# First attention: probabilities scaled on ScalarE, the score factor moved into the queries' evictions

## The chip, the cores and the metric

The kernel runs on one core of a Trainium2 chip. The metric is the device time of one execution in microseconds. A run of one execution more was taken with the hardware profiler; all rows below are from it.

## The reference, cut to what matters

Four decoder layers run one after the other on x (4 sequences of 256 tokens, width 512) with a context of 64 tokens for each sequence. The change touches the first attention only:

```python
hidden = jnp.concatenate([context, latents], axis=1)
q = (latents @ Wq.T).reshape(b, q_len, H, HD)          # 16 heads of 96
k = (hidden @ Wk.T).reshape(b, s_len, KV, HD)          # 4 key heads, 320 keys
v = (hidden @ Wv.T).reshape(b, s_len, KV, HD)
scale = 1.0 / jnp.sqrt(jnp.asarray(HD, q.dtype))
scores = jnp.einsum('bkgqd,bksd->bkgqs', q, k) * scale
attn = jax.nn.softmax(scores.astype(jnp.float32), axis=-1).astype(q.dtype)
out = jnp.einsum('bkgqs,bksd->bkgqd', attn, v)
```

Later layers (feed-forwards, two more kinds of attention, two mixtures of experts, and a last feed-forward whose weights are first quantised to a table of 16 values) are computed by code that stays as it is.

## The kernel before

All work is written as one list of steps (`schedule`), and every engine walks this list in its order, doing its own part of each step and waiting on semaphores for the others. No engine overtakes: what stands behind a waiting instruction waits too.

The first attention is cut into 64 units of one head and one sequence (256 queries, two tiles of 128, by 320 keys). Eight stages hold 8 units each: four groups of heads for the first two sequences, then for the other two. Unit n goes through a pipeline over four steps of the list:

- `scores0` n: TensorE multiplies queries by keys into two PSUM banks. VectorE takes the negated maximum of each row of both (L1192), multiplies the two maxima by the factor HD0 ** -0.5 (L1195, a 128x2 operation) and marks `max0`. ScalarE waits for that mark, then takes the exponential of both banks with the same factor as its scale (L936), writes `e0`, and accumulates the row sums in `sm`.
- `scale0` n stands one unit later, behind `scores0` n + 1. VectorE takes the reciprocal of the two sums (L1200) and multiplies the two tiles of `e0` in place by it (L1202, 128x320 each), marking `probs0`.
- `turn0` n stands behind `scores0` n + 2: TensorE transposes the probabilities (L1718, L1719), and ScalarE copies them out of PSUM to `eT0` (L944, L946).
- `pv0` n stands behind `scores0` n + 3: TensorE multiplies by the values (L1728). ScalarE writes the rounded high part of the result over the queries in `q0` (L888, 96x256), and VectorE the low part, which is the rest (L1118, 96x256). The low part waits for the high part.

Between the units stand the projections of the next stage: the queries (`q0`, four products of 12 matrix multiplications with 512 columns, evicted as a high part by ScalarE, L888 96x512, and a low part by VectorE, L1118 96x512), the keys, and the output projection of the stage before (`o0`, added to x on L1214). A stage's first two or three units have no projection of queries beside them, so TensorE has least to do there.

Two kinds of other work are woven in. The first is the splitting of weights into a high part (ScalarE, L903) and a low part (POOL, L813, 2 to 2.6 us each). The second is the quantisation of the last layer's weights, named `nf`: VectorE makes steps of a staircase (L1581 `nf_y`, L1575, L1591), which TensorE sums (L1977). Their places in the list are fixed by counting costs that the change leaves alone.

TensorE's banks go round a ring of 7, and a bank is claimed again only after its last reader. In the light units the transpose of unit n claims the banks of the scores of unit n + 1, whose last readers are the exponentials of that unit.

Of the kernel before, what the change touches and what calls it, by code (L numbers as in the profile page):

```python
# [5 lines left out]
FP32 = mybir.dt.float32  # L6
F32R = mybir.dt.float32r
INT32 = mybir.dt.int32
ALU = mybir.AluOpType
ACT = mybir.ActivationFunctionType  # L10
# [11 lines left out]
TPB = S // P  # L22
H0, G0, HD0 = 16, 4, 96
HPG = H0 // G0
KEYS0 = S + CTX
# [14 lines left out]
E0_RING = 5  # L40
# [308 lines left out]
def build(nc, a, out, known, only=None):  # L349
    ctx = ExitStack()  # L350
    with ctx:
        sig = Signals(nc, ctx, known)

        def sb(name, shape, dt, scope=ctx):
            return scope.enter_context(nc.sbuf_tensor(name, shape, dt))
# [13 lines left out]
        mx = sb("mx", [P, 4, 2 * HPC], FP32)  # L369
        sm = sb("sm", [P, 4, 2 * HPC], FP32)  # L370
# [13 lines left out]
        q0 = sb("q0", [HD0, 2, 2, HPG, HALF], F32R, s0)  # L384
        k0 = sb("k0", [HD0, 2, 2, BPH, KEYS0], F32R, s0)
        v0 = sb("v0", [P, TPH + BPH, G0 * HD0], FP32, s0)
        eT0 = sb("eT0", [P, 2, 3, S], FP32, s0)
        e0 = sb("e0", [P, E0_RING, KEYS0], FP32, s0)
# [78 lines left out]
        def psum(key):  # L467
            return banks[sig.bank_for(key)]
# [133 lines left out]
        if known:  # L602
            last = known.last_step
            free_after = {}
            slot_of, n = {}, 0
# [45 lines left out]
        slot_no, n = {}, 0  # L651
# [13 lines left out]
        def weight(name, part):  # L665

            _, p, dims, _, dest, _ = chunks[chunk_no[name]]
            if dest is not None:
                return dest[part]
            size = int(np.prod(dims))  # L670
            return flat(slots[0:p, slot_no[name] % NSLOT, part, 0:size], dims)
# [118 lines left out]
        def split_source(i):  # L790
            _, p, dims, *_ = chunks[i]
            return flat(staging[0:p, i % 2, 0:int(np.prod(dims))], dims)
# [3 lines left out]
        def _(pool):  # L796
# [12 lines left out]
            def split(i):  # L809
                pool.wait_ge(*sig.when("weight_high", i))  # L810
                _, p, dims, *_ = chunks[i]
                hi, lo = weight(chunks[i][0], 0), weight(chunks[i][0], 1)
                g.tensor_tensor(lo, split_source(i), hi.bitcast(FP32), ALU.subtract).then_inc(*sig.mark("weight_low", i))  # L813
# [68 lines left out]
        def _(act):  # L882
            sc = nc.scalar

            def high(stage, key, dst, src, product=None, func=ACT.Copy, **kw):

                act.wait_ge(*sig.when(*(product or (f"{stage}_product", key))))
                sc.activation(dst, src, func, **kw).then_inc(*sig.mark(f"{stage}_high", key))  # L888
# [37 lines left out]
                high("kc0", s, k0[:, s % 2, 0, :, S:], psum(("kc0", s))[0:HD0, 0:BPH * CTX].rearrange("p (b n) -> p b n", b=BPH))  # L926

            def q0_(s, h):
                high("q0", (s, h), q0[:, s % 2, 0, h], psum(("q0", s, h))[0:HD0])

            def scores0(n, s, bl, h):
                act.wait_ge(*sig.when("max0", n))
                for i in range(TPB):
                    if 2 * n + i >= E0_RING:
                        act.wait_ge(*sig.when("turn0_product", (2 * n + i - E0_RING) // 2))
                    sc.activation(e0[:, (2 * n + i) % E0_RING], psum(("scores0", n, i))[:, 0:KEYS0], ACT.Exp, scale=HD0 ** -0.5,  # L936
                                  bias=mx[:, n % 4, 2 + i:3 + i], accum_out=sm[:, n % 4, i:i + 1])\
                        .then_inc(*sig.mark("exp0", (n, i)))

            def turn0(n, s, bl, h):  # L940
                act.wait_ge(*sig.when("turn0_product", n))
                if n >= 2:
                    act.wait_ge(*sig.when("pv0_product", n - 2))
                sc.activation(eT0[:, n % 2, 0:2], psum(("turn0", n, 0))[:].rearrange("p (k n) -> p k n", k=2),  # L944
                              ACT.Copy).then_inc(*sig.mark("turn0_kept", (n, 0)))
                sc.activation(eT0[0:CTX, n % 2, 2], psum(("turn0", n, 1))[0:CTX, 0:S],  # L946
                              ACT.Copy).then_inc(*sig.mark("turn0_kept", (n, 1)))
# [136 lines left out]
            def nf_turn(m):  # L1084
                for i in range(2):
# [3 lines left out]
                    elif i == 0:  # L1089
                        act.wait_ge(*sig.when("nf4_max", (0, 0)))  # L1090
                    sc.activation(nf_t[0:88, i], psum(("nf_turn", m))[0:88, i * P:(i + 1) * P], ACT.Copy)\
                        .then_inc(*sig.mark("nf4_turned", (m, i)))

            handlers = {"split": split, "turn": turn, "v0": v0_, "k0": k0_, "kc0": kc0_, "q0": q0_, "scores0": scores0,
                        "turn0": turn0, "pv0": pv0, "up0": up0, "down0": down0, "scores1": scores1, "pv1": pv1, "bias2": bias2,
                        "route1": route1, "router1": router1, "zt1": zt1, "k2": k2_, "m2": m2_, "c2": c2_,
                        "gate2": gate2, "moe": moe, "hid2": hid2, "k3": k3_, "v3": v3_, "q3": q3_,
# [7 lines left out]
        def _(dve):  # L1105
            v = nc.vector
            links = [0]

            def link(ins):

                links[0] += 1
                ins.then_inc(sig.sem("vector_chain"), 1)
                dve.wait_ge(sig.sem("vector_chain"), links[0])

            def low(stage, key, dst, src, hi):

                dve.wait_ge(*sig.when(f"{stage}_high", key))
                v.tensor_tensor(dst, src, hi.bitcast(FP32), ALU.subtract).then_inc(*sig.mark(f"{stage}_low", key))  # L1118
# [65 lines left out]
                    psum(("kc0", s))[0:HD0, 0:BPH * CTX].rearrange("p (b n) -> p b n", b=BPH), k0[:, s % 2, 0, :, S:])  # L1184

            def q0_(s, h):
                low("q0", (s, h), q0[:, s % 2, 1, h], psum(("q0", s, h))[0:HD0], q0[:, s % 2, 0, h])

            def scores0(n, s, bl, h):
                for i in range(TPB):  # L1190
                    dve.wait_ge(*sig.when("scores0_product", (n, i)))
                    ins = v.tensor_reduce(mx[:, n % 4, i:i + 1], psum(("scores0", n, i))[:, 0:KEYS0], AX.X, ALU.max,  # L1192
                                          negate=True)
                link(ins)
                v.tensor_scalar(mx[:, n % 4, 2:4], mx[:, n % 4, 0:2], HD0 ** -0.5, None, ALU.mult)\  # L1195
                    .then_inc(*sig.mark("max0", n))

            def scale0(n):
                dve.wait_ge(*sig.when("exp0", (n, TPB - 1)))
                link(v.reciprocal(sm[:, n % 4, 2:4], sm[:, n % 4, 0:2]))  # L1200
                for i in range(TPB):
                    v.tensor_scalar(e0[:, (2 * n + i) % E0_RING], e0[:, (2 * n + i) % E0_RING], sm[:, n % 4, 2 + i:3 + i], None, ALU.mult)\  # L1202
                        .then_inc(*sig.mark("probs0", (n, i)))

            def pv0(n, s, bl, h):
                cs = slice(bl * S, (bl + 1) * S)
# [377 lines left out]
            def nf_end(n, m, f):  # L1584
# [3 lines left out]
                if m == 2:  # L1588
                    o, code, i1 = o.rearrange("p (q r) -> p r q", r=4), code.rearrange("p (r q) -> p r q", r=4), \
                        i1.rearrange("p (r q) -> p r q", r=4)  # L1590
                v.scalar_tensor_tensor(o, code, float(STAIR_SCALE), i1, ALU.mult, ALU.mult).then_inc(*sig.mark("nf4_dequantised", n))  # L1591

            handlers = {"stats": stats, "turn": turn, "k0": k0_, "kc0": kc0_, "q0": q0_, "scores0": scores0,
                        "scale0": scale0, "scale3": scale3, "pv0": pv0, "o0": o0, "up0": up0, "down0": down0, "scores1": scores1,
                        "pv1": pv1, "router1": router1, "route1": route1, "z1": z1, "zt1": zt1, "b1": b1, "k2": k2_,
                        "m2": m2_, "bias2": bias2, "gate2": gate2, "moe": moe, "hid2": hid2, "out2": out2,
                        "values3": values3, "scores3": scores3, "pv3": pv3, "o3": o3, "up3": up3,
                        "down3": down3, "nf_max": nf_max_, "nf": nf, "nf_end": nf_end}
# [463 lines left out]
```

## Time and profile before

| what | value |
|---|---|
| median of 3 runs | 1707.35 us (1707.07 to 1708.24) |
| the profiled execution | 1711.2 us, its span 1709.4 us |
| TensorE busy | 1443.9 us, 84% of the span |
| VectorE busy | 1083.9 us, 63% |
| ScalarE busy | 458.6 us, 27% |
| POOL busy | 296.5 us, 17% |
| mean granted TensorE clock | 0.893 |
| the units of the first attention | 65.8 us to 622 us of the span |

The span is the time from the first to the last instruction. TensorE is busy for most of it. The first attention takes a third of the span, and all that the change touches lies there. In the rows DVE is VectorE, ACT is ScalarE, PE is TensorE, and PEld its weight loads.

### The profile page before, as it was taken

To read this page: it belongs to the slowest core of one execution; us is meant where nothing else is said; L and a number is where in the kernel's file an instruction comes from. 1 tells how busy PE (TensorE), PEld (TensorE's weight loads), DVE (VectorE), ACT (ScalarE), POOL (GpSimd) and SP (SyncE) were. 2 spreads that over 40 slices of the span, in tenths; PEclk is the share of its full clock that TensorE was granted. 3 is DMA by queue.
4 is the path that set the end of the run, shared out by engine and by line. 5 is a ranking of instruction groups with operands and counts; after the bars stand their busy time and mean duration, and the time that the engine had idled before them with its cause. 6 is when DMAs were issued, how large, how long until landed. Compare 5 with 4: busy or idle time off the path is not lost.

```text
span 1709.4 us, 18898 instructions
## 1 busy us (share of the span) xinstructions
PE 1443.9 (84%) x6489; PEld 1131.2 (66%) x6489; DVE 1083.9 (63%) x2489; ACT 458.6 (27%) x994; POOL 296.5 (17%) x170
## 2 busy tenths in 40 slices
PE   6569999998999898899646878858999778789998
PEld 5347776776677667688545767747887546567786
DVE  4556876767777666948886756554446399944142
ACT  3223423332343333313131202101221333322010
POOL 4101111111111111202021002111543121012120
PEclk9779999999999999999855699557999889899999
DMA  5521232322232212222001112200112000001011
GB/s 184 159 77 46 80 82 68 82 74 58 64 89 71 75 50 69 72 66 67 25 26 46 42 40 60 63 18 1 50 49 62 26 25 1 1 27 60 16 36 49
DMA packets 99407, 96.40 MB, mean 56 GB/s; under 512 B 13138, under 2 KB 72418, under 8 KB 99314
## 3 DMA queue, kind: packets, MB, share of 16 engines
q1 hardware_dynamic: 98802, 94.35, 19.0%
q8 instruction: 54, 0.88, 0.2%
q0 software_dynamic: 512, 0.85, 0.2%
q14 instruction: 39, 0.32, 0.1%
HBM read 84.34 MB, written 10.82 MB: 56 GB/s over the span
## 4 chain that ended last, share of the span: by engine, by line
PE 62%; DVE 25%; issue 4%; ACT 4%; DMA 2%; SPq 1%; POOL 1%; DVEq 0%; ACTq 0%; POOLq 0%
PE bank L1636 48%; PE bank L1977 5%; PE bank L1728 4%; DVE nf_y L1581 3%; DVE st L1141 2%; DVE xn L1159 1%; PE bank L1661 1%; DVE xT L1118 1%; PE bank L1718 1%; DVE mx L1192 1%; DVE mx L1498 1%; ACT e L936 1%; DMA nf_w<-in_L_w 1%; DVE sm L1510 1%; SPq L767 1%
## 5 line engine op out<-in xcount | busy, mean ns | idle before, releaser
L1636 PE MATMUL bank<-xT,slots 128*128 128x512 f32 (+1 forms) x1920 | 467.6, 402 | 9.6 <-DVE xT L1118 7.8
L1636 PEld LDWEIGHTS bank<-xT,slots 128*128 128x128 f32 (+1 forms) x1920 | 354.8, 186 | 109.0 <-issue 8.9
L813 POOL TENSOR_TENSOR slots<-staging,slots 128x1024 fp32r<-128x1024 f32 (+4 forms) x97 | 230.5, 2379 | 1103.0 <-ACT slots L903 1103.0
L1581 DVE TENSOR_SCALAR nf_y<-nf_w 128x512 fp32r<-128x512 f32 (+2 forms) x495 | 232.2, 496 | 29.0 <-PE bank L1977 28.0
L1636 PE MATMUL bank<-slots,h 128*128 128x512 f32 (+1 forms) x728 | 178.8, 405 | 20.1 <-DVE h L1248 13.9
L1977 PE MATMUL bank<-nf_y,nf_d 128*128 128x512 f32 (+2 forms) x495 | 170.6, 429 | 10.3 <-DVE nf_y L1581 8.0
L1636 PEld LDWEIGHTS bank<-slots,h 128*128 128x128 f32 (+1 forms) x728 | 140.8, 194 | 56.1 <-DVE h L1248 14.8
L903 ACT ACTIVATE slots<-staging 128x1024 fp32r<-128x1024 f32 (+4 forms) x97 | 98.1, 1018 | 189.9 <-PE bank L1636 174.2
L936 ACT ACTIVATE e<-bank,mx 128x320 f32<-128x320 f32 x128 | 66.4, 523 | 271.1 <-DVE mx L1195 254.0
L1977 PEld LDWEIGHTS bank<-nf_y,nf_d 128*128 128x128 f32 (+1 forms) x495 | 95.3, 197 | 47.0 <-issue 15.5
L1214 DVE TENSOR_TENSOR x<-bank,x 128x512 f32<-128x512 f32 x72 | 49.7, 690 | 110.9 <-PE bank L1636 110.6
L1728 PE MATMUL bank<-eT,v 128*96 128x256 f32 (+1 forms) x384 | 112.0, 414 | 1.5 <-ACT eT L946 1.5
L1118 DVE TENSOR_TENSOR q<-bank,q 96x256 fp32r<-96x256 f32 (+1 forms) x96 | 48.8, 508 | 77.3 <-ACT q L888 76.8
L1636 PE MATMUL bank<-slots,q 96*128 96x512 f32 x384 | 95.3, 397 | 0.7 <-DVE q L1118 0.7
L1718 PE MATMUL bank<-ident,e 128*128 128x128 f32 x256 | 50.6, 294 | 44.5 <-ACT e L936 22.4
L1636 PEld LDWEIGHTS bank<-slots,q 96*128 96x128 f32 x384 | 71.6, 188 | 18.6 <-issue 2.1
L1728 PEld LDWEIGHTS bank<-eT,v 128*96 128x96 f32 (+1 forms) x384 | 58.2, 172 | 37.6 <-issue 25.3
L1661 PE MATMUL bank<-ident,xn 128*128 128x128 f32 x256 | 49.6, 360 | 31.9 <-DVE xn L1159 31.6
L1636 PE MATMUL bank<-k,q 96*128 96x320 f32 x384 | 69.6, 317 | 5.7 <-ACT e L936 4.4
L1718 PEld LDWEIGHTS bank<-ident,e 128*128 128x128 f32 x256 | 35.0, 151 | 53.7 <-ACT e L936 30.6
L1636 PEld LDWEIGHTS bank<-k,q 96*128 96x128 f32 x384 | 61.9, 192 | 13.0 <-ACT e L936 4.7
L1661 PEld LDWEIGHTS bank<-ident,xn 128*128 128x128 f32 x256 | 42.8, 189 | 39.2 <-issue 34.7
(246 smaller groups left out, 1897.8 us busy)
## 6 DMA issues: line engine op xcount, KB each, us to landing
staging<-in_L_wqkT SPq DMA_DIRECT2D x16, 480.0 KB, 3.8
nf_out<-nf_w SPq DMA_DIRECT2D x30, 256.0 KB, 2.1
staging<-nf_out SPq DMA_DIRECT2D x30, 256.0 KB, 2.8
staging<-in_L_woT SPq DMA_DIRECT2D x16, 384.0 KB, 3.5
staging<-in_L_w SPq DMA_DIRECT2D x12, 512.0 KB, 4.0
nf_a<-nf_max SPq DMA_DIRECT2D x40, 128.0 KB, 3.6
nf_r<-nf_rcp SPq DMA_DIRECT2D x40, 128.0 KB, 3.4
nf_w<-in_L_w SPq DMA_DIRECT2D x15, 256.0 KB, 4.4
```

The lines of the kernel that those rows point to most:

```text
L813: g.tensor_tensor(lo, split_source(i), hi.bitcast(FP32), ALU.subtract).then_inc(*sig.mark("weight_low", i))
L903: sc.activation(weight(name, 0), split_source(i), ACT.Copy).then_inc(*sig.mark("weight_high", i))
L936: sc.activation(e0[:, (2 * n + i) % E0_RING], psum(("scores0", n, i))[:, 0:KEYS0], ACT.Exp, scale=HD0 ** -0.5, bias=mx[:, n % 4, 2 + i:3 + ...
L1118: v.tensor_tensor(dst, src, hi.bitcast(FP32), ALU.subtract).then_inc(*sig.mark(f"{stage}_low", key))
L1141: ins = v.bn_stats(st[:, t], x[:, t])
L1214: v.tensor_tensor(x[:, t], src, x[:, t], ALU.add).then_inc(*sig.mark(*mark))
L1581: v.tensor_scalar(nf_y[0:rows, i % STAIR_RING, 0:size], w_, bound, first, compare, ALU.mult)\
L1636: ins = mm(dst, l_, r_, start=i == 0, stop=i == len(passes) - 1)
L1661: ins = nc.tensor.transpose(bank[:, i * P:(i + 1) * P], xn[:, i, c * P:(c + 1) * P], ident[:])
L1718: nc.tensor.transpose(b0[:, (2 * k + i) * P:(2 * k + i + 1) * P], e0[:, (2 * n + i) % E0_RING, k * P:(k + 1) * P], ident[:])
L1728: ins = mm(bank[0:HD0, 0:S], v0[0:p, t, g * HD0:(g + 1) * HD0], eT0[0:p, n % 2, k], start=k == 0, stop=k == 2)
L1977: mm(banks[NF_BANK][0:rows, 0:size], nf_d[0:rows, j - 1, 0:rows], nf_y[0:rows, i % STAIR_RING, 0:size], start=j == 1, stop=j == NPART).the ...
```

## The change

Four things differ. ScalarE's eviction of the queries multiplies by HD0 ** -0.5, and VectorE's low part of the queries does the same in one operation with two steps, so that the scores come out of the product already scaled. The 128x2 multiplication of the maxima is gone, and the second maximum itself marks `max0`. The exponential has no scale any more. VectorE keeps only the reciprocal of `scale0` and marks `sums0`, and ScalarE multiplies the two tiles of `e0` in place (new function `scale0`, with a factor per row as the scale of a copy).

```diff
             def q0_(s, h):
-                high("q0", (s, h), q0[:, s % 2, 0, h], psum(("q0", s, h))[0:HD0])
+                high("q0", (s, h), q0[:, s % 2, 0, h], psum(("q0", s, h))[0:HD0], scale=HD0 ** -0.5)
...
-                    sc.activation(e0[:, (2 * n + i) % E0_RING], psum(("scores0", n, i))[:, 0:KEYS0], ACT.Exp, scale=HD0 ** -0.5,
-                                  bias=mx[:, n % 4, 2 + i:3 + i], accum_out=sm[:, n % 4, i:i + 1])\
+                    sc.activation(e0[:, (2 * n + i) % E0_RING], psum(("scores0", n, i))[:, 0:KEYS0], ACT.Exp,
+                                  bias=mx[:, n % 4, i:i + 1], accum_out=sm[:, n % 4, i:i + 1])\
                         .then_inc(*sig.mark("exp0", (n, i)))
+
+            def scale0(n):
+                act.wait_ge(*sig.when("sums0", n))
+                for i in range(TPB):
+                    e = e0[:, (2 * n + i) % E0_RING]
+                    sc.activation(e, e, ACT.Copy, scale=sm[:, n % 4, 2 + i:3 + i]).then_inc(*sig.mark("probs0", (n, i)))
...
             def q0_(s, h):
-                low("q0", (s, h), q0[:, s % 2, 1, h], psum(("q0", s, h))[0:HD0], q0[:, s % 2, 0, h])
+                dve.wait_ge(*sig.when("q0_high", (s, h)))
+                v.scalar_tensor_tensor(q0[:, s % 2, 1, h], psum(("q0", s, h))[0:HD0], HD0 ** -0.5,
+                                       q0[:, s % 2, 0, h].bitcast(FP32), ALU.mult, ALU.subtract).then_inc(*sig.mark("q0_low", (s, h)))
...
-                link(ins)
-                v.tensor_scalar(mx[:, n % 4, 2:4], mx[:, n % 4, 0:2], HD0 ** -0.5, None, ALU.mult)\
-                    .then_inc(*sig.mark("max0", n))
+                ins.then_inc(*sig.mark("max0", n))
 
             def scale0(n):
                 dve.wait_ge(*sig.when("exp0", (n, TPB - 1)))
-                link(v.reciprocal(sm[:, n % 4, 2:4], sm[:, n % 4, 0:2]))
-                for i in range(TPB):
-                    v.tensor_scalar(e0[:, (2 * n + i) % E0_RING], e0[:, (2 * n + i) % E0_RING], sm[:, n % 4, 2 + i:3 + i], None, ALU.mult)\
-                        .then_inc(*sig.mark("probs0", (n, i)))
+                v.reciprocal(sm[:, n % 4, 2:4], sm[:, n % 4, 0:2]).then_inc(*sig.mark("sums0", n))
```

TensorE's and POOL's orders stay the same. On ScalarE, this is the order around unit 32 (the first unit of the fifth stage) before: the two exponentials of unit 32, the two copies of the transposed probabilities of unit 30, and the high part of the product with the values of unit 29.

```order
L936 ACTIVATE e0,sm<-bank2,mx 128x320
L936 ACTIVATE e0,sm<-bank3,mx 128x320
L944 ACTIVATE eT0<-bank4 128x512
L946 ACTIVATE eT0<-bank5 64x256
L888 ACTIVATE q0<-bank6 96x256
L903 ACTIVATE slots<-staging 128x960
```

The same place of the changed kernel:

```order
L936 ACTIVATE e0,sm<-bank2,mx 128x320
L936 ACTIVATE e0,sm<-bank3,mx 128x320
L944 ACTIVATE e0<-e0,sm 128x320 x2
L950 ACTIVATE eT0<-bank4 128x512
L952 ACTIVATE eT0<-bank5 64x256
L888 ACTIVATE q0<-bank6 96x256
L903 ACTIVATE slots<-staging 128x960
```

The two multiplications of unit 31's probabilities have come in between the exponentials and the evictions (L950 and L952 are the old L944 and L946).

On VectorE, this is the same unit before: the maxima of unit 32, a step of the staircase, the reciprocal of unit 31's sums, and the low part of unit 29's product with the values.

```order
L1192 TENSOR_REDUCE mx<-bank2 128x1
L1192 TENSOR_REDUCE mx<-bank3 128x1
L1195 TENSOR_SCALAR mx<-mx 128x2
L1581 TENSOR_SCALAR nf_y<-nf_w 128x512
L1200 RECIPROCAL sm<-sm 128x2
L1202 TENSOR_SCALAR e0<-e0,sm 128x320 x2
L1581 TENSOR_SCALAR nf_y<-nf_w 128x512
L1118 TENSOR_TENSOR q0<-bank6,q0 96x256
```

The same place of the changed kernel:

```order
L1200 TENSOR_REDUCE mx<-bank2 128x1
L1200 TENSOR_REDUCE mx<-bank3 128x1
L1584 TENSOR_SCALAR nf_y<-nf_w 128x512
L1206 RECIPROCAL sm<-sm 128x2
L1584 TENSOR_SCALAR nf_y<-nf_w 128x512
L1124 TENSOR_TENSOR q0<-bank6,q0 96x256
```

The multiplication of the maxima and the two of the probabilities are gone, and the reciprocal still stands behind a step of the staircase.

## Rows read from the trace of the kernel before

**Rows 1.** Busy time by stretch, us; light units 268:284, heavy ones 284:334, sum over 60:620

```profile
268.00:284.00 16.00, 12.75 (x61) 8.84 (x60) 14.13 (x32) 6.99 (x21) 4.39 (x2) 0.89 0.22 67
284.00:334.00 50.00, 50.00 (x246) 37.80 (x245) 34.49 (x85) 15.68 (x45) 4.23 (x2) 1.00 0.29 76
...
sum 560.00, PE 500.89 PEld 371.97 DVE 395.38 ACT 195.13 POOL 73.71; mean PE 26.36 PEld 19.58 DVE 20.81 ACT 10.27 POOL 3.88
```

**Rows 2.** The chain that ended last, units 40 and 41: start, us, what

```profile
429.54 0.18 DVE mx L1195
...
430.17 0.70 ACT e L936 x3
430.87 0.49 ACT eT L944
...
431.61 0.28 ACT q L888
...
431.91 0.42 DVE q L1118
```

**Rows 3.** The same chain: first and last of 16 short L1195, and of 5 long

```profile
84.53 0.18 DVE mx L1195
...
205.63 1.27 DVE mx L1195
...
500.68 1.82 DVE mx L1195
...
613.14 0.18 DVE mx L1195
```

**Rows 4.** The same chain: where it passes VectorE's scaling of e

```profile
69.76 0.68 DVE e L1202 x2
...
80.64 0.68 DVE e L1202 x2
```

**Rows 5.** VectorE's groups, 60:620: count, busy us, mean ns, idle before, releaser

```profile
L1581 DVE TENSOR_SCALAR nf_y<-nf_w 128x512 fp32r<-128x512 f32 x324 | 160.9, 520 | 10.7 <-PE bank L1977 9.9
...
L1202 DVE TENSOR_SCALAR e<-e,sm 128x320 f32<-128x320 f32 x128 | 43.7, 384 | 2.3
L1118 DVE TENSOR_TENSOR q<-bank,q 96x256 fp32r<-96x256 f32 x62 | 26.1, 421 | 54.4 <-ACT q L888 53.9
```

**Rows 6.** ScalarE's groups by shape, whole span, same columns

```profile
L888 ACT ACTIVATE xT<-bank 128x512 fp32r<-128x512 f32 x56 | 30.1, 599 | 26.3 <-PE bank L1661 26.1
L888 ACT ACTIVATE q<-bank 96x256 fp32r<-96x256 f32 x64 | 24.0, 375 | 3.3 <-PE bank L1728 3.1
...
L888 ACT ACTIVATE xT<-bank,lnw 128x512 fp32r<-128x512 f32 x8 | 5.4, 687 | 7.6 <-PE bank L1661 6.5 <-DMA lnw<-in_L_lnw 1.1
...
L920 ACT ACTIVATE v<-bank 128x384 f32<-128x384 f32 x8 | 3.7, 488 | 12.4 <-PE bank L1636 12.4
...
L1024 ACT ACTIVATE bqw<-bqf 128x512 fp32r<-128x512 f32 x1 | 0.6, 629 | 4.0 <-DVE bqf L1373 4.0
```

**Rows 7.** ScalarE in time: two 128x64 with a factor per row, together

```profile
955.16 0.59 ACT L1001 ACTIVATE r<-r,rs 128x64 f32<-128x64 f32 x2 [1.91 <-DVE rs L1330]
```

**Rows 8.** VectorE's groups, whole span: without and with a factor on the PSUM input

```profile
L1214 DVE TENSOR_TENSOR x<-bank,x 128x512 f32<-128x512 f32 x72 | 49.7, 690 | 110.9 <-PE bank L1636 110.6
...
L1216 DVE SCALAR_TENSOR_TENSOR x<-bank,x 128x512 f32<-128x512 f32 x8 | 5.5, 691 | 12.8 <-PE bank L1636 12.8
```

**Rows 9.** All engines in time, unit 32: start, us, what, idle before

```profile
335.80 2.57 POOL L813 TENSOR_TENSOR slots<-staging,slots 96x1024 fp32r<-96x1024 f32 x1 [16.78 <-ACT slots L903]
...
337.00 1.40 DVE L1195 TENSOR_SCALAR mx<-mx 128x2 f32<-128x2 f32 x1
...
338.31 0.41 DVE L1581 TENSOR_SCALAR nf_y<-nf_w 128x512 fp32r<-128x512 f32 x1
...
338.65 0.15 DVE L1200 RECIPROCAL sm<-sm 128x2 f32<-128x2 f32 x1
...
339.45 0.60 ACT L944 ACTIVATE eT<-bank 128x512 f32<-128x512 f32 x1
```

More of the change, by code:

```diff
@@ L1092, in nf_turn @@
                         .then_inc(*sig.mark("nf4_turned", (m, i)))
-            handlers = {"split": split, "turn": turn, "v0": v0_, "k0": k0_, "kc0": kc0_, "q0": q0_, "scores0": scores0,
+            handlers = {"split": split, "turn": turn, "v0": v0_, "k0": k0_, "kc0": kc0_, "q0": q0_, "scores0": scores0, "scale0": scale0,
                         "turn0": turn0, "pv0": pv0, "up0": up0, "down0": down0, "scores1": scores1, "pv1": pv1, "bias2": bias2,
```

## The prediction, made before the changed kernel was run

> **What bounds the kernel now.** I first read the busy time by stretch. TensorE is busy for 500.89 of the 560 us of the first attention, VectorE for 395.38, ScalarE for 195.13 [rows 1]. Taken over everything, ScalarE has plenty of room and VectorE is the busier of the two. But the stretches differ. In 284:334, a stage's heavy units with their projections, TensorE is busy for all 50.00 us, and neither engine is on the path. In 268:284, where a stage begins and TensorE has little to do, it is busy for 12.75 of 16 us, and the granted clock falls to 0.89. What VectorE and ScalarE cost the kernel, they cost there.
>
> So I read the chain of waits in those places next, piece by piece. Rows 2 are one crossing of it. VectorE multiplies the maxima, ScalarE does two exponentials, then the two evictions of the transposed probabilities, then the high part of the product with the values, and only then can VectorE do the low part, the staircase steps and the next maxima. From the end of L1195 at 429.72 to the start of L1118 at 431.91 the chain is on ScalarE for 2.19 us, and none of it on VectorE's scaling of e, which runs meanwhile. I counted how often the chain goes from L1195 to ScalarE in this way: 16 times with the short L1195 of 0.18 us, and 5 times with one of 1.27 to 1.82 us, 7.6 us together [rows 3]. VectorE's scaling of e stands on the chain in full only twice, 0.68 us each [rows 4].
>
> The group rows say the same over all units: VectorE sat idle for 54.4 us before 62 low parts, 53.9 of it for ScalarE's high part [rows 5]. That is 0.88 us in a unit. VectorE comes to this place early and waits for ScalarE.
>
> **The change part by part.**
>
> *Taken off VectorE.* The two scalings cost 2 x 0.34 us of its time in a unit (0.68 us for the pair [rows 4]), the multiplication of the maxima 0.18 us and a 0.02 us hand-over [rows 2]. Over 64 units that is 56 us. Where TensorE is the bound this is worth nothing. In the crossings the scaling is hidden behind ScalarE, and VectorE will only wait longer before L1118: about 0.88 + 0.68 + what is added on ScalarE. What does count there is the multiplication, since ScalarE waits for it: 0.20 us a crossing.
>
> *Put on ScalarE.* No row has this copy, so I build it. From PSUM with a constant scale, 256 columns take 375 ns and 384 take 488, so 320 take 431 [rows 6]. A factor per row adds 687 - 599 = 88 ns, and an input in SBUF in place of PSUM 629 - 599 = 30 ns [rows 6]: 549 ns for one. Back to back they overlap: two 340 ns operations of 128x64 with a pointer end in 0.59 us, so 90 ns are shared [rows 7]. That gives 0.46 us a copy, 0.92 us a pair. The lower bound is the PSUM form with a constant, overlapped: 0.34, a pair 0.68. The upper bound is 0.55 with no overlap: a pair 1.10. I take 0.92, since each addend has a row of its own.
>
> The Trainium skill, page "ScalarE: Activation LUTs", section "Rules for kernel authors", sends multiplications to VectorE, which speaks against the change. The rows agree for this shape: 0.34 us a tile on VectorE against my 0.46 on ScalarE.
>
> *Where the pair stands.* It is behind the exponentials and ahead of the evictions and of the high part that VectorE waits for. All of it lies on the chain in a crossing. Queued behind it are L950, L952, the high part on L888, and sometimes a split of weights, and POOL and the DMA queue wait for that. The new wait for `sums0` costs nothing in most units: the reciprocal stands behind one staircase step of about 0.34 us, and is done before the two exponentials are.
>
> *Short crossings.* 0.92 - 0.20 = +0.72 us. 16 of them: +11.5 us. In three of these, read further, the chain goes on to TensorE's transposes and not to an eviction. Three of the six transposes can run after the first copy, under most of the second's 0.46 us. I take off 3 x 0.33 = 1.0 us.
>
> *Long crossings.* Here L1195 was held. In rows 9 POOL's subtraction runs from 335.80 to 338.37, L1195 is issued at 337.00 and ends at 338.40, where the same instruction takes 0.18 us elsewhere. The rule in the Trainium skill, page "SBUF — State Buffer", section "Who interferes with whom", is that VectorE in a two-port mode and POOL lock each other out for a whole instruction. The trace agrees. By that rule alone one would say that all five holds come back.
>
> They don't, by the order: the next instruction on VectorE is a step of the staircase, and the reciprocal stands behind it. Such steps are held as well: their mean is 520 ns [rows 5], where one alone takes 0.41 us [rows 9]. In unit 32 the exponentials would start at about 337.0 and end at 338.0. The staircase step would still begin to move only when POOL ends, and the reciprocal end at about 338.80, as before. ScalarE then waits for it, copies until 338.82 + 0.92 = 339.74, and starts the eviction that before started at 339.45. That is +0.29 us. 5 of them: +1.5 us.
>
> *Pieces that go.* The 0.68 us at 80.64 goes. At 69.76 the pair goes too, but ScalarE must then do exponentials, copies and the next exponentials in a row, which takes the same time to about 0.1 us. Together -0.8 us.
>
> *The queries.* 32 evictions get a constant factor. On VectorE, 128x512 with a factor takes 691 ns against 690 without [rows 8]. Zero. The exponential loses an immediate: zero.
>
> **Sum:** 11.5 - 1.0 + 1.5 - 0.8 = +11.2 us, against the profiled execution 1711.2 + 11.2. Its own time is 3.9 us over the median of the runs, and I apply the difference to the median: 1707.35 + 11.2 = 1718.5 us. With a pair at 0.68: 16 x 0.48 - 1.0 + 5 x 0.05 - 0.8 = +6.1, 1713.5. With a pair at 1.10: 16 x 0.90 - 1.0 + 5 x 0.47 - 0.8 = +15.0, 1722.4. This case's own range is 1713 to 1723.
>
> **The rivals.**
>
> *The holds come back.* If the staircase step is not held where the multiplication was, for instance because POOL now starts later against it, the five long crossings give 0.92 - 0.20 - 1.34 (7.6 / 5 - 0.18) = -0.62 each instead of +0.29: 11.2 - 4.6 = +6.6, 1714. This is what the rule on the Trainium skill's page "SBUF — State Buffer" gives if it is applied to the multiplication alone. Against it: the same step is next in the order at unit 32, and POOL's start is set by ScalarE's split ahead of the unit. Chance 0.10.
>
> *No change.* ScalarE is busy for 195 of 560 us, and the copies vanish in its idle time. That is true of the heavy units. For the light ones it would need TensorE to be the later one at the crossings, and the chain says otherwise. With a pair near 0.68 and the holds back, 6.1 - 5 x (0.05 + 0.86) = +1.5 us: 1709. Chance 0.13.
>
> *Faster.* VectorE is the bound in the light units by its own work, and each of the 21 crossings gives back what was taken from it, 0.88 us: -18.5 us, 1689. It decides from the point where VectorE has no idle time ahead of L1118. For it: VectorE is busy for 14.13 of the 16 us in 268:284 [rows 1]. Against it: the 54.4 us [rows 5], and that rows 2 have ScalarE between two pieces of VectorE. Chance 0.08.
>
> *Slower still.* TensorE idles longer in each crossing and its clock falls more often. In 268:284 the clock of 0.89, with levels of 2.4 and 1.2 GHz, is 3.5 us of 16 at the lower one, and costs about 1.8 us. Four or five such falls more add 8 us: 1727. Chance 0.09.
>
> **How the numbers follow.** The forecast case has 0.60, all between 1713 and 1723. With the holds back (0.10) or the clock (0.09) it is slower too: slower 0.79, same 0.13, faster 0.08. Within 0.2%, 3.4 us, is about what a measurement of this kernel can't tell from no change. The range takes in the no-change case in part and the clock case: 1708.5 to 1727.
>
> **What would show it.** In the changed profile: new groups of 128 copies of about 550 ns on ScalarE's L944, and in pairs 1.0 us. VectorE's busy time down by about 56 us less holds, and its idle time before the 96x256 low parts up from 54.4 us to some 150 us (62 x 1.6 us more). ScalarE's busy time up by some 60 us. TensorE idle longer where the stages begin, and TensorE's busy time at the full clock unchanged. On the chain L944's copies 20 times or more, between the exponentials and the evictions. At unit 32, an idle time of ScalarE behind the exponentials that ends with the reciprocal. The prediction is wrong if the chain at the crossings shows VectorE's own work on both sides, if the copies come out below 0.3 us, or if the long `nf_y` steps shrink with the holds.

## The result, and the profile after

The changed kernel takes 1729.89 us (median of 4 runs, 1727.29 to 1736.76), the kernel before 1707.8 (4 runs, 1707.07 to 1708.97). The ratio is 1.0135, interval 1.0105 to 1.0165: slower by 22 us. The forecast was 1718.5, with a range up to 1727. The direction was right, the forecast difference was half of what came, and the result lies above the range.

The first thing to read is the busy time on the page of the profile, engine by engine.

```profile
span 1728.2 us, 18834 instructions
## 1 busy us (share of the span) xinstructions
PE 1453.3 (84%) x6489; PEld 1131.7 (65%) x6489; DVE 1027.8 (59%) x2297; ACT 516.4 (30%) x1122; POOL 296.0 (17%) x170
```

Before, the span was 1709.4, with TensorE (PE) busy for 1443.9, VectorE for 1083.9 and ScalarE for 458.6 us. VectorE is down by 56.1 and ScalarE up by 57.8, both as forecast. TensorE has the same 6489 instructions, and they take 9.4 us more. That was not forecast.

Next, where in the time. These are the rows of two stretches, the first attention and all that follows, of the kernel before (columns: stretch, length, busy time and instructions of TensorE, its weight loads, VectorE, ScalarE and POOL, granted clock, DMA share, GB/s).

```profile
60.00:622.00 562.00, 502.89 (x2403) 372.88 (x2403) 396.13 (x980) 195.62 (x539) 73.71 (x31) 0.94 0.27 75
622.00:1709.00 1087.00, 903.01 (x3907) 727.67 (x3906) 658.49 (x1452) 244.69 (x428) 202.35 (x124) 0.86 0.13 39
```

The same two of the changed kernel:

```profile
60.00:639.00 579.00, 515.03 (x2403) 376.31 (x2403) 339.91 (x788) 253.49 (x667) 72.79 (x31) 0.93 0.26 73
639.00:1728.00 1089.00, 901.70 (x3907) 726.26 (x3906) 658.69 (x1452) 244.66 (x428) 202.71 (x124) 0.86 0.13 39
```

What follows the attention is unchanged. The attention is 17 us longer, and TensorE is busy for 12 of them with the same 2403 matmuls, at 0.93 of the full clock instead of 0.94.

The groups that answer to [rows 5], from 60 to 640 us of the changed kernel (count, busy us, mean ns, idle before and what ended it):

```profile
L1584 DVE TENSOR_SCALAR nf_y<-nf_w 128x512 fp32r<-128x512 f32 x326 | 170.7, 547 | 9.4 <-PE bank L1980 8.7
...
L944 ACT ACTIVATE e<-e,sm 128x320 f32<-128x320 f32 x128 | 64.5, 555 | 12.3 <-DVE sm L1206 12.3
...
L1721 PE MATMUL bank<-ident,e 128*128 128x128 f32 x256 | 52.0, 299 | 48.7 <-ACT e L944 48.3 <-issue 0.4
...
L1124 DVE TENSOR_TENSOR q<-bank,q 96x256 fp32r<-96x256 f32 x64 | 26.9, 421 | 152.1 <-ACT q L888 152.1
```

The copy takes 555 ns. VectorE's idle time before its low parts went from 54.4 [rows 5] to 152.1 us, all of it ended by ScalarE. TensorE waits 48.3 us for the copies ahead of its transposes. Most of that is not new. Before, the same transposes waited 44.5 us, for the exponentials and for VectorE's scaling (from 60 to 640 us of the kernel before):

```profile
L1718 PE MATMUL bank<-ident,e 128*128 128x128 f32 x256 | 50.6, 294 | 44.5 <-ACT e L936 22.4 <-DVE e L1202 22.1
```

The steps of the staircase went from a mean of 520 to 547 ns.

A crossing on the chain that ended last (start, us, what), to be held against [rows 2]:

```profile
253.52 0.81 DVE mx L1200 x2
...
255.28 0.20 ACT e L936
255.48 0.90 ACT e L944 x2
256.38 0.49 ACT eT L950
256.87 0.26 ACT eT L952
257.13 0.27 ACT q L888
```

The piece of VectorE for the multiplication has gone, and the pair of copies stands in the chain with 0.90 us. On the whole chain L944 has 19.0 us, in 26 crossings, where the prediction had counted 21.

The same chain at unit 32, a place where the multiplication was held [rows 9]:

```profile
348.17 0.80 DVE mx L1200 x2
348.97 1.70 DVE nf_y L1584
350.68 0.08 DVE sm L1206
350.76 0.02 issue
350.78 0.02 ACT e L944
```

The staircase step is now held for 1.70 us in its place, and the copies wait for the reciprocal behind it.

Last, TensorE's clock at one place, the start of unit 25. First TensorE's timeline before (start, us, line, tiles, count, and the idle time ahead of it):

```profile
279.79 0.66 PE L1718 MATMUL bank<-ident,e 128*128 128x128 f32 x2 [1.86 <-ACT e L936]
...
281.10 2.41 PE L1728 MATMUL bank<-eT,v 128*96 128x256 f32 x6
283.43 3.03 PE L1636 MATMUL bank<-xT,slots 128*96 128x512 f32 x12
```

The same in the changed kernel:

```profile
288.91 0.66 PE L1721 MATMUL bank<-ident,e 128*128 128x128 f32 x2 [2.51 <-ACT e L944]
...
290.21 3.01 PE L1731 MATMUL bank<-eT,v 128*96 128x256 f32 x6
293.15 5.25 PE L1639 MATMUL bank<-xT,slots 128*96 128x512 f32 x12
```

The wait grew by 0.65 us, near what the chain owes for one crossing (0.92 - 0.20). But the clock, which before was back at 2.4 GHz for the twelve matmuls of the projection, was at 1.2 GHz in the changed kernel: 5.25 us where there were 3.03, and 3.01 where there were 2.41. In this execution the wait cost 0.65 us, and the matmuls behind it 2.8 more.

This is one execution, and not a rule for the place. In a second profile of the changed kernel (after_again below) the level fell one unit earlier, and the same twelve matmuls ran at 2.4 GHz:

```profile
292.82 3.02 PE L1639 MATMUL bank<-xT,slots 128*96 128x512 f32 x12
```

What both profiles of the changed kernel have is more time at the lower level around here: one stretch of 10.3 us in the first and one of 6.8 us in the second, against one of 3.4 us in each of the two profiles of the kernel before.

### The profile page after: what moved, and what is told of

The parts are those of the page before. It is cut to its first block, busy times and chain, and to the rows that moved or that the text cites. A ratio compares the mean times of both kernels' runs of the same rounds, so it can differ in the third digit from the quotient of the medians.

```text
span 1728.2 us, 18834 instructions
## 1 busy us (share of the span) xinstructions
PE 1453.3 (84%) x6489; PEld 1131.7 (65%) x6489; DVE 1027.8 (59%) x2297; ACT 516.4 (30%) x1122; POOL 296.0 (17%) x170
## 4 chain that ended last, share of the span: by engine, by line
PE 58%; DVE 26%; ACT 6%; issue 5%; DMA 2%; SPq 2%; POOL 1%; DVEq 0%; ACTq 0%
PE bank L1639 46%; PE bank L1980 5%; DVE nf_y L1584 4%; PE bank L1731 4%; DVE st L1147 2%; DVE xn L1165 1%; SPq L767 1%; DVE xT L1124 1%; PE bank L1664 1%; DVE mx L1200 1%; ACT e L936 1%; ACT e L944 1%; DVE mx L1501 1%; PE bank L1721 1%; DMA nf_a<-in_L_w 1%
## 5 line engine op out<-in xcount | busy, mean ns | idle before, releaser
L1639 PE MATMUL bank<-xT,slots 128*128 128x512 f32 (+1 forms) x1920 | 470.4, 403 | 11.3 <-DVE xT L1124 8.0
L1584 DVE TENSOR_SCALAR nf_y<-nf_w 128x512 fp32r<-128x512 f32 (+2 forms) x495 | 241.2, 514 | 28.6 <-PE bank L1980 27.6
L1639 PEld LDWEIGHTS bank<-slots,h 128*128 128x128 f32 (+1 forms) x728 | 141.0, 194 | 56.2 <-DVE h L1251 14.8
L1731 PE MATMUL bank<-eT,v 128*96 128x256 f32 (+1 forms) x384 | 116.7, 428 | 2.7 <-ACT eT L952 2.5
L1124 DVE TENSOR_TENSOR q<-bank,q 96x256 fp32r<-96x256 f32 x64 | 26.9, 421 | 152.1 <-ACT q L888 152.1
L1721 PE MATMUL bank<-ident,e 128*128 128x128 f32 x256 | 52.0, 299 | 48.7 <-ACT e L944 48.3
L944 ACT ACTIVATE e<-e,sm 128x320 f32<-128x320 f32 x128 | 64.5, 555 | 12.3 <-DVE sm L1206 12.3
```

The lines of the kernel that those rows point to most:

```text
L944: sc.activation(e, e, ACT.Copy, scale=sm[:, n % 4, 2 + i:3 + i]).then_inc(*sig.mark("probs0", (n, i)))
L1584: v.tensor_scalar(nf_y[0:rows, i % STAIR_RING, 0:size], w_, bound, first, compare, ALU.mult)\
L1639: ins = mm(dst, l_, r_, start=i == 0, stop=i == len(passes) - 1)
L1721: nc.tensor.transpose(b0[:, (2 * k + i) * P:(2 * k + i + 1) * P], e0[:, (2 * n + i) % E0_RING, k * P:(k + 1) * P], ident[:])
L1731: ins = mm(bank[0:HD0, 0:S], v0[0:p, t, g * HD0:(g + 1) * HD0], eT0[0:p, n % 2, k], start=k == 0, stop=k == 2)
```

## A way to split a difference

One profile is one execution. Each timed run also has its span and its mean granted clock. The clock has two levels, 1.2 and 2.4 GHz, so the time at the lower level is 2 x (1 - clock) x span. Half of it is the most that it can have cost in a run, as if TensorE had worked through all of it and everything had waited for TensorE. For a difference of two kernels half is an upper estimate and no strict bound, since the share of this time in which TensorE worked can differ too, and what is left is in the same way a lower estimate of the rest. The Trainium skill, page "TensorE: Matmul & The Clock Gate", section "HAM oscillation — how this bites in real kernels", prices lower-clock time by the same half. The twelve matmuls above, 5.25 against 3.03 us, come somewhat under it: 2.2 of 5.25 us, 0.42.

All means over the runs of each kernel, differences against the kernel before in the same comparison (for the changed kernel, against all 40 runs of before: span 1707.9, 358.7 us at the lower level; of the four in its own comparison only the profiled one has its clock on record, 0.893):

| kernel | runs | span | at the lower level | half of that | the rest |
|---|---|---|---|---|---|
| changed | 4 | +21.3 | +30.4 | +15.2 | +6.1 |
| factor_only | 10 | -3.6 | +9.9 | +5.0 | -8.5 |
| scaling_only | 4 | +27.5 | +26.3 | +13.2 | +14.4 |
| copies_last | 5 | +9.2 | +23.3 | +11.7 | -2.4 |
| dummy_320 | 4 | +30.4 | +26.1 | +13.1 | +17.4 |
| dummy_64 | 4 | +16.5 | +16.3 | +8.2 | +8.3 |
| act_heavy | 10 | -3.9 | -6.1 | -3.1 | -0.9 |
| act_light | 4 | +20.4 | +31.8 | +15.9 | +4.5 |
| before_fill | 10 | +7.2 | +5.2 | +2.6 | +4.6 |
| after_fill | 4 | +17.3 | +13.4 | +6.7 | +10.7 |

The time at the lower level has a standard deviation of 4 to 20 us over the runs of one kernel, so a half of it in the table is known to some 1 to 4 us, and to 5 in dummy_320. I worked this table out after the first eight kernels had run; their expectations don't speak of it.

Two readings say how far below the half the price lies. The first is from the traces of the attention, with the stretches at the lower level taken one by one. Before, TensorE was busy for 43.5 of the 64.9 us at the lower level in the first profile, and for 46.6 of 59.6 in the second. In the changed kernel it was busy for 62.0 of 84.4 and for 63.4 of 85.2. That is 17.6 us more of work at the lower level, and half of it is 8.8 us. The second is from the runs. Among the 99 runs of the table's kernels and the kernel before, each compared only with runs of its own kernel, a run with 1 us more at the lower level has a span 0.32 us longer (standard error 0.03). By that the 30.4 us of the changed kernel are worth 9.8 us. It is a relation between runs and not a test, but the two agree: an estimate of 9 to 10 us for the clock, which leaves 11 to 12 of the 21.3.

## The experiments

**factor_only: the factor moved into the queries, VectorE still scales.** The changed kernel with these lines put back on VectorE, and `scale0` taken off ScalarE:

```diff
-                v.reciprocal(sm[:, n % 4, 2:4], sm[:, n % 4, 0:2]).then_inc(*sig.mark("sums0", n))
+                link(v.reciprocal(sm[:, n % 4, 2:4], sm[:, n % 4, 0:2]))
+                for i in range(TPB):
+                    v.tensor_scalar(e0[:, (2 * n + i) % E0_RING], e0[:, (2 * n + i) % E0_RING], sm[:, n % 4, 2 + i:3 + i], None, ALU.mult)\
+                        .then_inc(*sig.mark("probs0", (n, i)))
```

> Only the factor is moved (scaled query evictions, no multiplication of the maxima); VectorE still scales the probabilities. Theory: ScalarE's pair of copies is the whole cost and the moved factor is a gain. Then each short crossing gives 0.20 us and each of the 5 long ones 1.54 us: 16 x 0.20 + 7.7 = 10.9 us less than before, 1697 us (1693 to 1703). Rival: the scaled evictions or the missing multiplication cost something themselves: at or above 1708 us.

Measured: 1705.89 us against 1707.32, ratio 0.9978 (0.9959 to 0.9996). It gains 1.4 us by the medians where 10.9 were expected. Two things are behind that, and how much each took is not separated. By the table the rest fell by 8.5 us, and the clock took up to 5.0 back. And the holds came to other steps. This is VectorE's staircase group, 60 to 620 us, in this kernel:

```profile
L1581 DVE TENSOR_SCALAR nf_y<-nf_w 128x512 fp32r<-128x512 f32 x326 | 171.8, 551 | 7.1 <-PE bank L1977 6.3
```

Before it was 160.9 us in 324 steps [rows 5]. The 10.9 us more are holds of POOL that had fallen on the multiplication. In the trace of before 8 of the 64 multiplications were held, 11.3 us beyond their usual 0.17 us each, and 22 steps took over 0.65 us. Here 29 steps did, each with POOL at work beside it.

**scaling_only: ScalarE scales, the multiplication of the maxima stays.**

```diff
                 dve.wait_ge(*sig.when("exp0", (n, TPB - 1)))
-                link(v.reciprocal(sm[:, n % 4, 2:4], sm[:, n % 4, 0:2]))
-                for i in range(TPB):
-                    v.tensor_scalar(e0[:, (2 * n + i) % E0_RING], e0[:, (2 * n + i) % E0_RING], sm[:, n % 4, 2 + i:3 + i], None, ALU.mult)\
-                        .then_inc(*sig.mark("probs0", (n, i)))
+                v.reciprocal(sm[:, n % 4, 2:4], sm[:, n % 4, 0:2]).then_inc(*sig.mark("sums0", n))
```

> Only the scaling of the probabilities is moved to ScalarE; VectorE still multiplies the maxima. Theory: it is worse than the whole change, by what the moved factor gives: 0.20 us in some 25 crossings plus holds of the multiplication, 1735 us (1731 to 1745). Rival, the factor's move is what costs: at or below 1712 us.

Measured: 1737.23 us, ratio 1.0156 (1.0128 to 1.0185). The two parts together make the change: by the ratios, 0.9978 and 1.0156 multiply to 1.0134, where 1.0135 was measured (by the medians, -1.4 and +29.9 sum to 28.5 against 22). The scaling is the loss, and the factor gives a little back.

**copies_last: the changed kernel, with the copies of unit n + 2 behind the high part of unit n.** They no longer hold up the evictions, but are ready later for TensorE. The copies of units 0 and 1 stay where they were.

```diff
                 high("pv0", n, q0[:, s % 2, 0, h, bl * S:(bl + 1) * S], psum(("pv0", n))[0:HD0, 0:S])
+                if n + 2 < 64:
+                    scale0(n + 2)
```

> The changed kernel with ScalarE's two copies of a unit behind the high part of the product with the values, instead of ahead of the evictions. The same work on each engine. Theory: the cost is what is queued behind the copies, above all the high part that VectorE waits for. Then the copies lie under VectorE's low part, staircase steps and maxima, and the time is near that of the factor alone, 1700 us (1694 to 1710). Rival: TensorE's transposes wait for the probabilities, which come no earlier (later, if anything): 1725 us or more.

Measured: 1718.46 us, ratio 1.0051 (1.0026 to 1.0076): between the two, so neither theory holds alone. About half of the loss is gone with the place in front of the evictions. What TensorE waits for, 60 to 640 us (us in total, times, longest):

```profile
PE bank L1727 <- ACT e L948: 46.7, 17, 13.1
```

It waits about as long as in the changed kernel (48.3) and as the kernel before in the same place (44.5). The rest in the table is even below zero, so what is left of the loss is by this estimate mostly clock (up to 11.7 us, known to some 4).

**dummy_320: the kernel before, with two unused copies of 128x320 on ScalarE in each unit, where the change puts its two.** VectorE still scales, and nothing on another engine waits for the added operations; only what is queued behind them on ScalarE does.

```diff
+            def dummy0(n):
...
+                for i in range(TPB):
+                    sc.activation(dm[:, i, 0:5], ident[:, 0:64].unsqueeze(1).broadcast_to((P, 5, 64)), ACT.Copy,
+                                  scale=ident[:, 0:1]).then_inc(sig.sem("dummy_done"), 1)
```

> The kernel before, with two more ScalarE operations of 128x320 with a factor per row in each of the 64 units, between the exponentials and the evictions, written to a buffer that nobody reads, and no wait of another engine on them. Theory: time on ScalarE at this place is the cost. 0.92 us in 21 to 25 crossings is 19 to 23 us, and the clock falls more often on top: 1732 us (1726 to 1742). Rival: the cost is the new hand-over from VectorE's reciprocal to ScalarE to TensorE; then this kernel is within 4 us of before, under 1712 us.

Measured: 1738.63 us, ratio 1.0181 (1.0147 to 1.0215). A crossing on its chain:

```profile
243.60 0.70 ACT e L937 x3
244.31 0.91 ACT dm L947 x2
245.21 0.48 ACT eT L954
```

The pair costs 0.91 us as it did in the change, and time on ScalarE at this place is enough to make the loss. The rest of +17.4 us is near the 21 crossings x 0.92 = 19.3 of the expectation, but the crossings are not fixed: on the chain of this profile the pair stands 36 times, with 32.1 us in all. Time that is added here brings further places onto the chain, each for a part of its length. The clock comes on top, up to 13.1. In the profiled execution, though, the clock was 0.896 (0.883 to 0.892 in the three others), and the attention had 64.9 us at the lower level, as the kernel before. Its span is still 23.7 us over that of the first profile of before. So the delay can cost this much by itself.

**dummy_64: the same with 128x64 in place of 128x320.** `dm[:, i, 0:5]` becomes `dm[:, i, 0:1]`.

> As the kernel with two unused 128x320 operations, but 128x64 each: a pair takes 0.59 us less 0.09 for the next, 0.49 us of ScalarE's time in place of 0.92. If the loss goes with ScalarE's time at this place: 0.49 / 0.92 of 31 us is 16.5 us, 1724 us (1718 to 1728). If the loss is mostly a falling clock that sets in only with long idle times: under 1716 us.

Measured: 1725.46 us, ratio 1.0107 (1.0068 to 1.0146). The loss follows the length of what is added: by the medians 17 us for the short pair and 31 for the long one. The group rows of the two kernels give the operations, this one first:

```profile
L947 ACT ACTIVATE dm<-ident 128x64 bf16<-128x64 f32 x128 | 37.1, 341 | 0.0
```

And of dummy_320:

```profile
L947 ACT ACTIVATE dm<-ident 128x320 bf16<-128x320 f32 x128 | 64.7, 557 | 0.0
```

**act_heavy and act_light: the factor in the queries as in the change, and ScalarE scales in a part of the units.** In act_heavy it scales the four of eight that come in the middle of a stage, where TensorE is the bound, and VectorE scales the others. act_light has it the other way round, with `not in`.

```diff
+def on_act(n):
+
+    return n % 8 in (2, 3, 4, 5)
...
             def scale0(n):
+                if not on_act(n):
+                    return
                 act.wait_ge(*sig.when("sums0", n))
```

> The changed kernel, but ScalarE scales only the units whose scaling falls beside projections (unit number modulo 8 from 2 to 5, 32 units); VectorE scales the other 32. Theory: beside projections TensorE is the bound and ScalarE's pair is free, so the time is that of the factor alone, 1706 us, plus at most 4. Rival, each of 64 pairs costs the same: half of the way from 1706 to 1730, 1718 us.

> The complement: ScalarE scales the units around the stages' boundaries (modulo 8: 6, 7, 0, 1), VectorE the others. Theory: here TensorE has little to do and the pair is on the chain, so nearly the whole loss is in these 32 units: 1726 us (1722 to 1731). Rival, every pair costs the same: 1718 us.

Measured: act_heavy 1705.58 us, ratio 0.9975 (0.9954 to 0.9997); act_light 1732.15, ratio 1.012 (1.0082 to 1.0159). Against factor_only, in which ScalarE scales nothing, scaling in the heavy units costs nothing that these runs can tell (0.9975 against 0.9978), and scaling in the light ones costs all. VectorE's 0.68 us a unit, taken off it where TensorE is the bound, buy nothing either, as the prediction said. act_light was some 6 us above its expectation and 1 above the range of it. Its time at the lower level is that of the changed kernel (+31.8 against +30.4), so the table doesn't explain the 6 us.

**after_again: the changed kernel once more, one profile.**

> The changed kernel once more, one look. If the part of the loss that is not TensorE's idle time is the granted clock, the span less TensorE's busy time is again 275 us (within 3), and what differs from 1728.2 us of span goes with TensorE's busy time and the granted clock.

Measured: 1727.9 us, span 1726.2. TensorE was busy for 1458.7 us, which leaves 267.5: a miss. So the split of a single profile into TensorE's busy and other time is only good to some 7 us (9.4 and 9.4 in the first profile, 14.8 and 2.0 here, both against the first profile of before). What was steady is the time at the lower level inside the attention, summed from 72 stretches of 8 us each: 84.9 and 85.3 us in the changed kernel's two profiles.

**before_again: the kernel before once more, one profile.**

> The kernel before once more, one profile. If the split of a profile into time at the lower level and the rest is steady enough to argue from: between 60 us and the end of the first attention 65 us at the lower level, plus or minus 5, where the changed kernel had 85 twice.

Measured: 1708.39 us; 59.7 us at the lower level in the attention, 65.0 in the first profile. It is within the bound, just. The changed kernel has 20 to 26 us more. TensorE was busy for 1440.9 us of a span of 1706.6, so the time other than busy is 265.7, and 265.5 in the first profile. By the means of the two profiles of each kernel the changed one has 13.6 us more of busy time and 5.6 more of the other. The busy time is not the clock alone: dummy_320 has 5.3 us more of it in the attention, with the clock as before.

**after_fill and before_fill: TensorE given work in its waits.** Both kernels got eight unused transposes ahead of the wait for the probabilities, in the first two units of seven stages; the real ones overwrite what they write.

```diff
                 b1_ = claim(("turn0", n, 1), ("turn0_kept", (n, 1)))
+                if n >= 8 and n % 8 < 2:
+                    for i in range(8):
+                        nc.tensor.transpose(b0[:, i % 4 * P:(i % 4 + 1) * P], ident[:], ident[:])
                 for i in range(TPB):
```

> The changed kernel with eight unused transposes of the identity on TensorE (about 1.5 us of work) ahead of its wait for the probabilities in the first two units of seven of the eight stages, where the trace of after shows waits of 0.2 to 2.5 us; the real transposes overwrite what they write. Theory (half of the loss is the clock that falls behind these idle times): the time at the lower level between 60 us and the end of the first attention falls from 85 us to 70 or less, and the kernel gains 5 to 10 us: 1720 to 1725. Rival (the clock falls for another reason, or the loss is the delay alone): the time is that of the changed kernel or up to 5 us more, 1728 to 1735, since the added work only runs into the wait or past it.

> The kernel before with the same eight unused transposes in the same units. Theory (idle time at these crossings makes the clock fall, less often than in the changed kernel): the time at the lower level, 65 us in the first attention, falls by 10 or less, and the kernel's time is within 5 us of the kernel before, since its waits are shorter and the added work runs past some of them: 1703 to 1712. Rival (added work at the crossings costs its own time, whatever the clock): 14 units by up to 1.5 us, up to 20 us more.

Measured: after_fill 1727.21 us, ratio 1.0101 (1.0081 to 1.0122); before_fill 1715.74, ratio 1.0041 (1.0022 to 1.0061). TensorE's timeline in after_fill, at the start of unit 25 again:

```profile
288.94 1.07 PE L1720 MATMUL bank<-ident 128*128 128x128 f32 x8 [0.43 <-ACT e L936]
289.85 0.38 PE L1724 MATMUL bank<-ident,e 128*128 128x128 f32 x2
...
290.54 1.68 PE L1734 MATMUL bank<-eT,v 128*96 128x256 f32 x6
292.15 3.03 PE L1639 MATMUL bank<-xT,slots 128*96 128x512 f32 x12
```

Here the clock is up: transposes at 0.38 and not 0.66 us, six matmuls at 1.68 and not 3.01, twelve at 3.03 and not 5.25. But at this place that is no proof of the filling. The level had been down one unit earlier, from 283.0 to 286.4 us, and in after_again, with nothing filled, the twelve took 3.02 us behind such an earlier fall. What counts is the sum: in the attention, the time at the lower level fell from 85 to 68.2 us, as the theory said. In time the kernel gained 2.7 us by the medians, under the 5 to 10 expected (1.0101 for 1.0135 as ratios, with intervals that overlap). The added work costs too: before_fill is 5.5 us slower than before by the medians, and at 1715.7 above my 1712. Its time at the lower level in the attention, which I expected to fall from 65 us by 10 or less, was 71.7 us: it rose. So neither kernel came where the theory had it, and by themselves they decide little. The pair tells more: with the same filling on both sides the change costs 1727.21 - 1715.74 = 11.5 us, and without it 22. In the table the rest differs by 6.1 between the two filled kernels (10.7 - 4.6), as it does without filling, and the clock's half by 4.1 (6.7 - 2.6) where it was 15.2. In the profiles, the attention of after_fill is 10.0 us longer than that of before_fill (580.7 and 570.7), and 0.9 of it is TensorE's busy time. So what the filling takes out of the difference is the clock. It does so from both sides: it lowers the time at the lower level in the changed kernel, and raises it in the kernel before.

## Why the prediction was low

**What held.** That ScalarE, and not VectorE, is on the path in the crossings: dummy_320 loses more than the change (31 us) with VectorE's scaling left in place. That only the light units count: act_heavy and act_light. The copy, 549 ns estimated and 555 measured, and the pair, 0.92 and 0.90 to 1.01. The Trainium skill, page "ScalarE: Activation LUTs", section "What ACT_TABLE_LOAD costs", has 280 ns + 0.833 ns a column for one with a pointer operand; an estimate from it for the copy is 280 + 0.833 x 320 = 547 ns. The 0.833 ns a column agrees with the two dummies, (557 - 341) / 256 = 0.84. The 56 us off VectorE, the some 60 on ScalarE, the idle time of about 150 before the low parts. In the long crossings, that the hold passes to the staircase step and the reciprocal ends behind it.

**The sum of +11.2 us** is that of the chain. The table's rest is 6.1 us, a lower estimate. With the clock at 9 to 10 us, 11 to 12 are left, and the two filled kernels differ by 11.5. So the sum is about right, or up to 5 us too high; I can't place it closer. That it comes so near is in part luck, since its count of crossings was not right. Of the five long ones only four go on to ScalarE: the one at 205.63 [rows 3] goes on over VectorE's own steps. And in the changed kernel the copies stand in 26 crossings on the chain, not in 21, with 19.0 us, part of them with one copy or less.

**The step that failed** is that the clock was left out of the sum. It stood only as the rival "Slower still. TensorE idles longer in each crossing and its clock falls more often", with a chance of 0.09 and 8 us, and nothing was said for so low a chance. It was no alternative to the chain's delay but came on top of it, and it should have been a term of the sum. The change adds 30.4 us at the lower level over a run. That is at most some 15 us of time, and 9 to 10 by the two readings above; with the chain's 11 to 12 it makes the 21 of the table. By the profiles 20 to 26 us of it lie in the attention. There both things happened. The level fell at places where it had not before, the starts of the second and the seventh stage, in both profiles (at about 152 and 512 us). And where it had fallen before, around unit 25, it stayed down longer, 10.3 and 6.8 us against 3.4. The price of 8 us for four or five new falls came near the size, though only a part of it is new falls. The sign that I gave, "TensorE's busy time at the full clock unchanged", told nothing, since the time that counts was not at the full clock.

**A smaller point.** "TensorE waits for copies" was in the sum only for three crossings and with a minus sign. TensorE waits 48.3 us for them, but it had waited 44.5 at this place before, so that only 4 are new. copies_last, which freed the evictions, kept 46.7 of the wait and half of the loss. I read this as two costs of the same copies, being ahead of the evictions and being late for the transposes; against factor_only, whose transposes wait 35.8 us, the second is larger than 4.

**What stays open.** Why one longer wait leads to a long stretch at the lower level and another doesn't; the rows show the stretches, but no run here was made to find the condition. And how far the clock would go with all waits filled: my filling covered 14 of them.

## What to carry to other kernels

An engine that is busy for a third of the time can be the one on the path. Read the chain at the places where TensorE waits, and see there which engine is early; moving work to the late one costs up to its full length at every crossing, and adds crossings, while moving it where TensorE was the bound cost nothing here. Then ask what the matmuls behind each lengthened wait will take at the lower clock level, and put that into the sum: here it nearly doubled the price of the change, and by the table took up to 5 of 8.5 us of a gain in factor_only. To look at it, use the granted clock of many runs; one profile is too few.

The best here are factor_only and act_heavy, both 0.2% under the kernel before, hardly outside their intervals, and the same as each other.

## What I had not expected of the hardware

- **Slightly longer waits, much more time at the lower clock.** In one execution 0.65 us more of a wait at unit 25 went with 2.8 us more in the 18 matmuls behind it (3.01 against 2.41, 5.25 against 3.03). In another of the same kernel the fall came a unit earlier, and the twelve took 3.02. The place moves from one execution to the next, while the sum in the attention moves less: 84.9 and 85.3 us in two profiles of the changed kernel, 65.0 and 59.7 before.
- **Holds don't go away with the instruction that is held.** With the 64 multiplications gone, of which 8 had been held for 11.3 us in all, the staircase steps took 10.9 us more (factor_only against [rows 5]). The rule of the Trainium skill, page "SBUF — State Buffer", section "Who interferes with whom", is that VectorE in a two-port mode and POOL lock each other out for whole instructions. The trace agrees, POOL being at work beside each of the 29 held steps, and adds that here the wait passed to the staircase step that VectorE issued next.
